# Layer-1 attention: where the projections, the second norm and the spreading of q and k stand in each engine's order

## What is computed

```
h        = layernorm(x)                    # first norm
q, k, v  = h @ WQ + bQ, h @ WK + bK, h @ WV + bV      # 16 heads of 16
scores   = q k^T / 4, causal window of 128
ao       = softmax(scores) @ v ;  attn_out = ao @ WO + bO
states   = scan(A, h @ Bw) ;      ssm_out  = states @ Cw
g        = sigmoid(h @ Wg + bg)
x1       = x + g * attn_out + (1 - g) * ssm_out
out      = x1 + gelu(layernorm(x1) @ W1 + b1) @ W2 + b2   # second norm, MLP
```

## Time and profile before

| what | value |
|---|---|
| median of three runs | 5119.75 us |
| the profiled execution's own time | 5103.98 us |
| its span, first to last instruction | 5102.1 us |
| busy share of the span: PE / DVE / ACT / POOL | 83% / 59% / 48% / 45% |
| mean granted TensorE clock | 0.942 |
| this phase's sequences | from about 2715 us to 4768 us |

### The profile page before, as it was taken

How to read it: one execution, slowest core, us unless ns; L and a number is a source line. 1 busy time by engine, 2 the same in 40 slices (tenths; PEclk the granted TensorE clock), 3 DMA queues, 4 the chain that set the end, 5 groups by cost and what they waited for, 6 DMA issues and landing times. The chain is left out here.

```text
span 5102.1 us, 148706 instructions
## 1 busy us (share of the span) xinstructions
PE 4251.0 (83%) x61044; PEld 3324.1 (65%) x61140; DVE 2991.0 (59%) x7226; ACT 2461.1 (48%) x5553; POOL 2307.9 (45%) x2391
## 2 busy tenths in 40 slices
PE   3888888888888858888886888888888888888558
PEld 2776776677667747777774666666666666666557
DVE  3777767777677657677764444444444444444346
ACT  3555545545545423323224555555555555555335
POOL 4665656666666500000004554444555444554364
PEclk8999999999999989999998999999999899999659
DMA  2222212222221110000001000000000000000233
GB/s 84 49 49 60 67 43 52 70 49 52 66 57 45 46 54 22 20 25 17 25 29 41 9 9 9 9 9 9 9 9 9 9 9 9 9 9 5 79 121 117
DMA packets 152048, 188.15 MB, mean 37 GB/s; under 512 B 28253, under 2 KB 112352, under 8 KB 149984
## 3 DMA queue, kind: packets, MB, share of 16 engines
q1 hardware_dynamic: 144528, 160.98, 11.8%
q0 software_dynamic: 6864, 17.99, 1.0%
HBM read 68.48 MB, written 44.19 MB: 22 GB/s over the span
## 5 line engine op out<-in xcount | busy, mean ns | idle before, releaser
L1569 POOL TENSOR_TENSOR c_prob<-c_prob,c_inv 128x512 f32<-128x512 f32 (+1 forms) x512 | 482.3, 949 | 750.3 <-DVE c_inv L1822 740.5
L1652 ACT ACTIVATE c_prob<-c_s_ps,c_nmax 128x256 f32<-128x256 f32 (+1 forms) x1024 | 454.8, 454 | 288.5 <-DVE c_nmax L1817 286.6
L1817 DVE TENSOR_REDUCE c_nmax<-c_s_ps 128x2 f32<-128x512 f32 (+1 forms) x512 | 317.2, 620 | 362.7 <-PE c_s_ps L2019 358.0
L848 POOL TENSOR_TENSOR a_swap<-a_swap,a_sin 128x512 f32<-128x512 f32 x128 | 206.5, 1613 | 555.5 <-DMA a_swap<-a_raw 555.4
L212 POOL TENSOR_TENSOR b_var<-b_mv,b_eps 128x4 f32<-128x4 f32 x16 | 8.5, 533 | 696.6 <-DVE b_mv L304 696.5
L2031 PE MATMUL c_t_ps<-c_ident,c_prob 128*128 128x128 f32 x1792 | 310.5, 290 | 13.3 <-POOL c_prob L1569 11.8
L889 ACT COPY a_raw<-a_w_ps 128x512 f32<-128x512 f32 x256 | 150.3, 587 | 339.9 <-PE a_w_ps L74 339.3
L1663 ACT COPY c_pT<-c_t_ps 128x512 f32<-128x512 f32 (+1 forms) x512 | 277.2, 541 | 50.1 <-PE c_ab_ps L2049 50.1
L1170 PE MATMUL a_w_ps<-a_mem,a_sT 64*32 64x65 f32 x14848 | 216.4, 226 | 96.0 <-issue 92.6
L2019 PE MATMUL c_s_ps<-c_k,c_q 64*128 64x256 f32 (+1 forms) x1024 | 250.1, 325 | 21.5 <-issue 18.0
L1170 PEld LDWEIGHTS a_w_ps<-a_mem,a_sT 64*32 64x32 f32 x14848 | 170.6, 106 | 147.6 <-issue 128.6
(11 more groups left out here) (377 smaller groups left out, 13760.7 us busy)
## 6 DMA issues: line engine op xcount, KB each, us to landing
a_swap<-a_raw SPq DMA_DIRECT2D x1024, 64.0 KB
d_xb<-sorted_rows SPq DMA_DIRECT2D x71, 130.0 KB
a_x_ln<-x SPq DMA_DIRECT2D x128, 64.0 KB, 2.1
a_acc<-x SPq DMA_DIRECT2D x64, 128.0 KB
after_attn<-a_acc SPq DMA_DIRECT2D x64, 128.0 KB, 2.4
b_x_in<-after_attn SPq DMA_DIRECT2D x16, 512.0 KB, 4.5
after_ffn<-b_acc SPq DMA_DIRECT2D x16, 512.0 KB, 3.2
c_x_in<-after_ffn SPq DMA_DIRECT2D x16, 512.0 KB, 4.7
```

Of the source, the lines that this page charges most:

```text
L848: nc.gpsimd.tensor_tensor(q_sw, q_sw, table(sin), ALU.mult)
L1569: nc.gpsimd.tensor_tensor(p, p, inv[:, n % 4].unsqueeze(2).to_broadcast([P, 2, KB])[:, :, keys_of(i)], ALU.mult).then_inc(norm_ready, 1)
L1652: last = nc.scalar.activation(prob[:, n % 4, h, keys_of(i)], s_ps[:, n % 2, h, keys_of(i)], ACT.Exp, bias=nmax[:, n % 4, h:h + 1], accum_o ...
L1817: nc.vector.tensor_reduce(nmax[:, n % 4], s_ps[:, n % 2, :, keys_of(i)], AX.X, ALU.max, negate=True).then_inc(max_ready, 1)
```

## The change

No instruction is added or removed; all three parts move work or its PSUM bank.

1. Projections rotate over four banks: the four results of `queries_keys` and the four of `values_gates` go to `ab_ps[1]`, `ab_ps[0]` and the two banks of `s_ps`, which are idle between the last exponential and the MLP's second product. The order is q1, q0, k1, k0 (the number is the half of the features).
2. The second norm moves: on VectorE `stats2_of` of the last tokens and `norm2` stand ahead of the last `qk_lo`, `h2n_of` behind the first `values_gates`. On TensorE `state_input` stands ahead of `h2_transposes`, and `values_gates` 2 and 3 behind it.
3. The first three spreading pairs (`HELD = 3`) of the next sequence stand inside the MLP, in `o_ps` (q) and `c_ps` (k): pair 0 ahead of `mlp1(0)`, pair 1 behind `mlp1(1)`, pair 2 between `mlp2(6)` and `mlp2(7)`. The other five stay at the first scores, with `scores(n)` now ahead of pair n + 4. The gates' tanh moves between `ff_hi(6)` and `gelu(7)`. `scores(0)` waits for two of four results, not for all.

```diff
+        s_bank = [s_ps[:, k].rearrange("p h k -> p (h k)") for k in range(2)]
+        in_ps = [ab_ps[:, 1], ab_ps[:, 0], s_bank[0], s_bank[1]]
+        in_order = ((0, 1), (0, 0), (1, 1), (1, 0))
+        HELD = 3
+        q4_ps = [o_ps[:] if j < HELD else ab_ps[:, 0] for j in range(PAIRS1)]
+        k4_ps = [c_ps[:].rearrange("p a d -> p (a d)") if j < HELD else ab_ps[:, 1] for j in range(PAIRS1)]
...
                 for c in range(DC):
                     h2_hi(it, c)
+                if not last_step(it):
+                    q4_copy(it + 1, 0)
                 for m in range(MF):
                     gelu(it, m)
                     ff_hi(it, m)
+                    if not last_step(it):
+                        if m == 0:
+                            q4_copy(it + 1, 1)
+                        if m == MF - 2:
+                            gates(it + 1)
+                if not last_step(it):
+                    q4_copy(it + 1, 2)
+                    nc.scalar.activation(table[:], b1[:, 0:1], ACT.Exp)
...
                 for n in range(NS + 1):
-                    if n + 2 < PAIRS1:
-                        k4_copy(it, n + 2)
                     if n < NS:
                         maxima(it, n)
+                    if HELD + 1 + n < PAIRS1:
+                        k4_copy(it, HELD + 1 + n)
                     if n:
                         inverse_sums(it, n - 1)
...
             def values_gates(it, t):
-                if t < 2:
-                    pe.wait_ge(qlo_ready, (it * 2 + 1) * DC + 2 - t)
-                else:
-                    pe.wait_ge(vg_ready, it * T + t - 1)
+                pe.wait_ge(qlo_ready, it * 2 * DC + t + 1)
...
-                if n == 0:
+                if n == 0 and not first_step(it):
+                    pe.wait_ge(result_ready, it * T - T // 2)
+                elif n == 1:
                     after(pe, result_ready, it * T)
...
                 if m < 2:
-                    pe.wait_ge(vg_ready, (it + 2) * T if not last_step(it) else NSEQ * T)
+                    if not last_step(it):
+                        pe.wait_ge(vg_ready, (it + 1) * T + 2)
...
                     values_gates(it + 1, 0)
                     values_gates(it + 1, 1)
-                    values_gates(it + 1, 2)
-                h2_transposes(it)
-                if not last_step(it):
-                    values_gates(it + 1, 3)
                     state_input(it + 1)
+                h2_transposes(it)
+                if more:
+                    values_gates(it + 1, 2)
+                    values_gates(it + 1, 3)
+                    spread_qk(it + 1, 0)
                 mlp1(it, 0)
                 mlp1(it, 1)
+                if more:
+                    spread_qk(it + 1, 1)
                 for m in range(MF):
                     mlp2(it, m)
                     if m + 2 < MF:
                         mlp1(it, m + 2)
+                    if more and m == MF - 2:
+                        spread_qk(it + 1, 2)
```

More of the change, by code:

```diff
@@ L1702, in _ @@
             projections(0)
+            for j in range(HELD):
+                q4_copy(0, j)
+            gates(0)
+            nc.scalar.activation(table[:], b1[:, 0:1], ACT.Exp)
             def body(it):
[L1705 to L1709, removed]
+                q4_copy(it, HELD)
                 for n in range(NS + LAG_T):
-                    if n + 2 < PAIRS1:
-                        q4_copy(it, n + 2)
+                    if HELD + 1 + n < PAIRS1:
+                        q4_copy(it, HELD + 1 + n)
                     if n < NS:
@@ L1790, in values_gates @@
                 heads = lambda ap: ap.rearrange("p (h e) -> p h e", e=DH1)
-                nc.vector.tensor_tensor(v[:, t, :, 0:DH1], heads(ab_ps[:, t % 2, 0:D]), heads(rows[:, 0]), ALU.add)
-                nc.vector.tensor_tensor(gate[:, t], ab_ps[:, t % 2, D:2 * D], rows[:, 1], ALU.add).then_inc(vg_ready, 1)
+                nc.vector.tensor_tensor(v[:, t, :, 0:DH1], heads(in_ps[t][:, 0:D]), heads(rows[:, 0]), ALU.add)
+                nc.vector.tensor_tensor(gate[:, t], in_ps[t][:, D:2 * D], rows[:, 1], ALU.add).then_inc(vg_ready, 1)
             def k4_copy(it, j):
@@ L1884, in _ @@
                 h_lo(0, c)
-            qk_lo(0, 0, 1)
-            projections(0, 0)
-            projections(0, 1)
+            for part in in_order:
+                qk_lo(0, *part)
+            for t in range(T):
+                values_gates(0, t)
+            scan(0)
+            for j in range(HELD):
+                k4_copy(0, j)
             def body(it):
                 order.step(it)
-                k4_copy(it, 0)
-                k4_copy(it, 1)
+                more = not last_step(it)
+                k4_copy(it, HELD)
                 for n in range(NS + 1):
-                    if n + 2 < PAIRS1:
-                        k4_copy(it, n + 2)
                     if n < NS:
                         maxima(it, n)
+                    if HELD + 1 + n < PAIRS1:
+                        k4_copy(it, HELD + 1 + n)
                     if n:
@@ L2096, in _ @@
                 h_transposes(0, c)
-            for a, m in ((0, 1), (0, 0), (1, 1), (1, 0)):
-                queries_keys(0, a, m)
+            for n in range(2 * DC):
+                queries_keys(0, n)
             for t in range(T):
@@ L2101, in _ @@
             state_input(0)
+            for j in range(HELD):
+                spread_qk(0, j)
             def body(it):
-                spread_qk(it, 0)
-                spread_qk(it, 1)
+                more = not last_step(it)
+                spread_qk(it, HELD)
                 for n in range(NS + LAG_P):
-                    if n + 2 < PAIRS1:
-                        spread_qk(it, n + 2)
                     if n < NS:
                         scores(it, n)
+                    if HELD + 1 + n < PAIRS1:
+                        spread_qk(it, HELD + 1 + n)
                     if LAG_T <= n < NS + LAG_T:
```

90 lines of the change are left out of this document (51 added, 39 removed).

## The result

| what | before | after |
|---|---|---|
| median of four runs | 5121.99 us | 4853.06 us |
| lowest and highest | 5115.79 to 5136.19 | 4848.22 to 4860.51 |
| profiled execution's own time | 5103.98 | 4853.39 |

The ratio is 0.9478, 95% interval 0.9447 to 0.9509: faster by 5.2%. Forecast were 4912 us and a range of 4872 to 4975, so the time lies 59 us under the forecast and 19 us under the range.

A forecast was written before the change was run, and what follows sets the result against it. TensorE was taken to set the end, its idle time being winnable. Savings of 8.0 + 0.7 + 0.1 + 4.4 = 13.2 us for 15 transitions, plus 2, took 5103.98 to 4904; adding 8 gave 4912 us, range 4872 to 4975.

The forecast's parts named there:

- B: Stretch from the MLP's start to the first `mlp2`: 4.46 us to become 3.75, saving 0.7, with the clock at full level.
- C: Stretch from the first `mlp2` to the MLP's end, 20.74 us: 0.1 saved, with pair 2 filling a wait.
- the gates' tanh: On ScalarE in the MLP: its 1.05 us fits the 1.46 idle ahead of the last gelu.
- Rival 1: ScalarE and VectorE queues delay first scores and the clock stays low after the MLP's start: 4978 us; chance 0.12.
- rival 2: The second norm comes no earlier, hanging on x1 or GpSimd, not VectorE's order: 4987 us; chance 0.03.
- A: Stretch from the first projection to the MLP: 25.57 us to become 17.6, saving 8.0.
- D: Stretch from the MLP's end through spreading and first scores to first values: 14.45 us to become 10.05, saving 4.4.
- the lower bound: Total if every named wait and some restarts vanished: 15.4 us saved for each transition between sequences, 4873 us.
- 200 us of the schedule: Saving over the phase: 13.2 us for each of 15 transitions, 198 us, plus 2 in the prologue.
- rival 3: The clock falls more often at the bias additions, say three more falls of 14.7 us each: 4956 us; chance 0.08.
- The rule that was weighed: Cycling through PSUM banks with brief idle times can make TensorE's clock oscillate; it spoke against the change, no size given.
- Rival 4: A clock fall at the bias additions in every body, and low clock after the MLP's start: 5158 us, slower; chance 0.02.

The follow-up runs named there:

- e4_norm_back: Changed kernel with the second norm's sums behind value blocks 0 and 1 and the state input behind the transposes, as before the change; 5066.48 us.
- e1: The kernel before, unchanged, run and profiled once more; median of ten 5127.68 us.
- e2: The changed kernel, unchanged, run and profiled once more; 4870.34 us.
- e11: The changed kernel, unchanged, run and profiled a third time, on another chip; 4863.12 us.
- e10_before_bias_out: Kernel before with gates' tanh between the last two gelus, gate scaling in the MLP, bias additions ahead of the first normalisation; 5085.37 us beside 5124.67, ratio 0.9929.
- e9: Changed kernel with the state input's six matmuls done twice in each body; 5020.3 us beside 4863 of the changed kernel.
- e5: Changed kernel with the projections in the two banks of ab_ps again and the waits this needs; 4978.8 us.
- e3: Changed kernel with spreading pairs 0 to 2 and their copies behind the MLP instead of inside it; 4992.1 us against 4870.
- e14: Changed kernel with the state input's six matmuls done three times in each body; 5074.22 us.
- run 50: Not a run's label: the lowest run of e9, 4914 us, was 50 us higher than the changed kernel's lowest.

## Why the forecast was short, point by point

**What held.** The cut of a body at TensorE's waits and the reading that the second norm was queued and not late: `e4_norm_back` shows it. The mechanism was right, and so was its size: every stretch came within 0.5 us of its forecast. The norm was there when TensorE came, as worked out, with 0.4 us to spare. B's clock stayed full, C changed by nothing, the gates' tanh was covered. Stores were to be 113 us apart and are 112.65; the first values were to come 52 us behind the first projection and come at 51.5. Rival 1 (the queues take it back) and rival 2 (the norm hangs on x1) did not occur.

**The step that failed** is the one from the schedule to the run: "The shown median lies 15.8 above that execution; I add half of it, since I read it as the clock's bad luck, told below, which can come or not". It is the start of the sum that was mis-sized, not a term of the schedule. The sum started from one profiled execution that held a fall of 16.9 us, kept it, and added 8 for more. It also took that execution's other phases as given, a term put at nothing without a reason. The changed kernel has no long fall in three profiles, and its runs scatter by 12 to 21 us where those of before scatter by 20 to 63. Of the 59 us between forecast and result, 16.9 + 8 = 25 are the falls kept and added; 7.5 are the sizes of A and D (0.5 us in 15 bodies) and the ends of the loop; 26 are the untouched phases, which differ by as much between executions of one kernel (`e1`, `e2`, `e11`). That the time came out under the range, and not just under the forecast, is the 16.9 and the 26: the lower bound, 4873, had 15.4 us saved in a body where 13.7 came, but nothing for either. The 200 us of the schedule were no luck, since the stretches agree one by one; the 26 us are chance. Beside the later runs they are smaller: there the changed kernel took 4863 and 4870, 10 and 17 us more, of which before, 3 and 12 us slower, had a part too.

**How it should have been read.** The row was there: clock 0.50 behind the scores that wait for the bias additions, in one body of fifteen. I made a rival of it (rival 3, more falls, 0.08) and none of its opposite, that a kernel whose profile shows one fall may lose it, and whatever its median holds beyond that. The runs showed that opposite: none in the changed kernel. `e10_before_bias_out` shows that 39 us of the median of before can be had by moving the bias additions and what stands with them, though not how many falls they were.

**The rule that was weighed.** In the rows of `e9` and `e5` falls begin at waits of 0.73 us, though most such waits pass without one. By the Trainium skill (TensorE: Matmul & The Clock Gate, "A second HAM failure mode: psum-queue depth-cycling") brief idle times between groups can make the clock oscillate: the rows agree on the idle times. On the banks they do not: the changed kernel rotates over four and had no long fall, `e5` over two and had three. I applied it to the wrong kernel, by its banks and not by its idle time. The changed one idles less and had none in 45 bodies, and `e3`, `e5` and `e9`, each a small step away from it, fell in 5, 3 and 8 of 15 bodies. Rival 4, a slower kernel by falls in every body, did not occur here; `e9` shows falls in every second body, at 14 and 35 us each.

**What stays open.** It is open why bodies of 112.65 us, with the wait still in them, were never hit in 45, while 114.0, 114.2, 115.4 and 117.2 were hit often, and 120.2 and 126.3 once each (in 15 and 30). In `e9` hit bodies alternate with whole ones, in `e14` five stand in a row, and executions of one kernel differ by up to 230 us. What decides it, no run here shows. Each part undone brought falls, but so did added work with all parts in place, so the changed kernel's freedom from them is not secured by its three parts. What removed them wherever it was tried is the edit that moves gate scaling and bias additions. That it works by the wait and not by the other things it moves is the likely reading, since all 24 falls begin there, but the two were not parted.

## What to carry to other kernels

Cut one period of the loop at the waits of the engine that sets the end, and ask of each wait whether its work was late or only queued: stretches can then be worked out to half a microsecond from the rows of before. Then look at the granted clock of every period, not of one: a period that is 10% longer with the same instructions is a fall, and the median can hold more or fewer of them than the profiled execution. Start a forecast from the usual period and not from one execution's total, and give the phases that stay alone the scatter that two profiles of one kernel show. Here a wait of 0.73 us was followed by a loss of 14 to 35 us in the bodies that were hit, so look at such waits first, and measure small edits without them.

## What the runs showed of the hardware that was not expected

- The clock fell from 2.4 to 1.2 GHz at a wait of 0.73 us while TensorE was otherwise busy, and was still low after 70 us of unbroken work (`e9`, 3114 to 3184 us; 149.1 us for a body of 114.0).
- With six matmuls more in each body, 21 us of work in all, the median was 157 us higher and the lowest run 50; with the bias additions moved away the same six made bodies of 113.45 in place of 112.0, 22 us in 15 of them, and no fall.
- Layer 0 and the feed-forward phase, the same instructions in all kernels, ended anywhere between 2676 and 2718 us.
